# A decoder of two layers on one core: the late stage in groups of four, two and two batches in place of four and four, the second attention's scores in two PSUM banks in place of three

## The reference

```
x = layernorm(x + attn0(x))          # 16 heads of 64, softmax, out projection
x = layernorm(x + xattn0(x, ctx))    # one head of 128, softmax, biases
x = layernorm(x + ffn0(x))           # tokens @ We + be, times the best gate's probability
x = layernorm(x + attn1(x))          # 16 heads of 8, causal softmax, out projection
x = layernorm(x + xattn1(x, ctx))    # rotated q and k, scores * decay mask, no softmax
x = layernorm(x + ffn1(x))           # inner 512, silu(gate) * up, down
```

## Time and profile before

| | |
|---|---|
| median of 3 runs | 333.19 us (332.2 to 333.38) |
| the profiled execution | 330.77 us, its span 329.0 us |
| busy share of the span | TensorE 76%, VectorE 66%, ScalarE 45%, GpSimd 20% |
| mean granted clock of TensorE | 0.902 of full |

### The profile page before, as it was taken

The page is one execution under the profiler, slowest core; times in us unless marked ns, Lnnn a source line. Parts: engine busy times, 40 slices in busy tenths (PEclk is TensorE's granted clock), DMA queues, the critical chain, the costliest instruction groups (busy, mean ns, idle before and its releaser), DMA issues.

```text
span 329.0 us, 6840 instructions
## 1 busy us (share of the span) xinstructions
PE 250.3 (76%) x2655; PEld 190.5 (58%) x2658; DVE 216.4 (66%) x538; ACT 148.2 (45%) x274; POOL 67.0 (20%) x102
## 2 busy tenths in 40 slices
PE   0858688988999989799967899999886667652430
PEld 0836567878787878687845566666564434240110
DVE  3996995679657996865356656567476756354662
ACT  5864662275437736144422354543525552202651
POOL 8900000000011001171114681352020002021002
PEclk9989999999999999999978999999999995655555
DMA  7985541344133502436000620004000000000011
GB/s 235 388 224 165 121 102 66 115 96 114 66 106 88 130 3 85 130 103 100 2 1 0 134 26 2 0 18 90 0 3 2 1 2 0 0 0 1 0 32 32
DMA packets 27679, 22.86 MB, mean 69 GB/s; under 512 B 19136, under 2 KB 24256, under 8 KB 26944
## 3 DMA queue, kind: packets, MB, share of 16 engines
q1 hardware_dynamic: 27648, 22.43, 25.9%
HBM read 12.20 MB, written 6.03 MB: 55 GB/s over the span
## 4 chain that ended last, share of the span: by engine, by line
PE 48%; DVE 28%; ACT 11%; issue 7%; POOL 3%; DMA 1%; ACTq 0%; DVEq 0%; POOLq 0%
DVE arena L1076 7%; PE PS L506 4%; ACT arena L883 3%; PE PS L683 3%; PE PS L579 3%; PE PS L606 3%; ACT xt L906 3%; PE PS L705 2%; DVE rowmax L1081 2%; PE PS L598 2%; PE PS L547 2%; POOL rstd L433 2%; PE PS L689 2%; PE PS L532 2%; PE PS L688 2%
## 5 line engine op out<-in xcount | busy, mean ns | idle before, releaser
L431 POOL TENSOR_SCALAR shift<-mv 128x3 f32<-128x3 f32 (+2 forms) x15 | 3.6, 240 | 243.2 <-DVE mv L1138 243.2
L1076 DVE TENSOR_TENSOR arena<-PS,arena 64x512 f16<-64x512 f32 x64 | 44.1, 690 | 6.7 <-ACT arena L883 5.1
L883 ACT ACTIVATE arena<-PS 64x512 f16<-64x512 f32 x64 | 37.8, 591 | 19.2 <-PE PS L534 18.4
L532 PE MATMUL PS<-xh,w0l 128*128 128x256 f32 x64 | 21.7, 339 | 17.0 <-DVE w0l L1067 9.5
L962 ACT ACTIVATE PT<-PS 128x512 f32<-128x512 f32 x32 | 19.1, 595 | 34.2 <-PE PS L689 34.1
L906 ACT ACTIVATE xt<-res,shift,rstd 128x128 f32<-128x128 f32 x42 | 17.7, 483 | 32.6 <-POOL shift L434 32.5
L1211 DVE TENSOR_REDUCE rowmax<-PS 128x4 f32<-128x512 f32 x32 | 21.9, 688 | 13.5 <-PE PS L691 13.1
L896 ACT ACTIVATE PT<-PS 128x512 f32<-128x512 f32 x32 | 19.1, 597 | 16.0 <-PE PS L563 14.5
L532 PEld LDWEIGHTS PS<-xh,w0l 128*128 128x128 f32 x64 | 13.4, 209 | 19.4 <-DVE arena L1076 9.7
L579 PE MATMUL PS<-V,PT 128*64 128x68 f32 x512 | 22.2, 229 | 1.9 <-DVE On L1105 1.9
L561 PE MATMUL PS<-arena 128*128 128x128 f16 x128 | 23.3, 221 | 0.3 <-DVE MR L1088 0.3
(11 more groups left out here) (206 smaller groups left out, 652.1 us busy)
## 6 DMA issues: line engine op xcount, KB each, us to landing
arena<-arena SPq DMA_DIRECT2D x8, 512.0 KB, 5.1
v_piece<-VN SPq DMA_DIRECT2D x8, 512.0 KB, 2.7
V<-v_piece SPq DMA_DIRECT2D x64, 64.0 KB, 2.5
arena<-k_piece SPq DMA_DIRECT2D x4, 192.0 KB, 4.4
arena<-q_piece SPq DMA_DIRECT2D x4, 192.0 KB, 6.3
q_piece<-VN SPq DMA_DIRECT2D x6, 96.0 KB, 1.7
xT<-x_T SPq DMA_DIRECT2D x1, 512.0 KB, 3.8
w<-wk SPq DMA_DIRECT2D x2, 256.0 KB, 4.6
```

The lines of the kernel that those rows point to most:

```text
L532: mm(dst, w0l[:, w, g], xh[:, x], start=True, stop=False)
L883: m = fn(dst[:, a], src[a * 64:(a + 1) * 64], ACT.Copy)
L1076: m = tt(lower[:, a], src[a * 64:(a + 1) * 64], upper[:, a], ALU.subtract)
```

## The change

Groups 3, 4 and 5 have four, two and two batches. Group 5 (batches 6 and 7) is now the last one, in which half of the batches are normalised by VectorE and the gate uses Silu; group 4 (batches 4 and 5) uses tanh, whose product takes one more VectorE instruction (L1242), and starts when the residuals of its own batches are there, while batches 6 and 7 are in the second attention. Its steps 0 to 11 use one PSUM bank, number 2, in two halves, which is why the scores are left with banks 0 and 1, and why V, which shares its half with K, moves from step 0 to step 2 and waits until VectorE has read K. Its first gate waits for the residual of batch 7. Group 5 uses banks 3 and 4. The buffers of group 4 in SBUF lie in tiles of the first attention and of the weights that are no longer read.

The diff, cut to what it does; each `LBANKS[g][i]` in the late steps becomes `LTILES[g][i]`, each `w % 3` a `w % 2`:

```diff
-N = (3, 3, 2, 4, 4)
-B0 = (0, 3, 6, 0, 4)
+N = (3, 3, 2, 4, 2, 2)
+B0 = (0, 3, 6, 0, 4, 6)
-MIDS, LATES = (0, 1, 2), (3, 4)
+MIDS, LATES = (0, 1, 2), (3, 4, 5)
...
-        LBANKS = {3: (5, 6, 7), 4: (4, 0, 1)}
+        LTILES = {3: (PS[:, 5, :], PS[:, 6, :], PS[:, 7, :]),
+                  4: (PS[:, 2, 0:TP], PS[:, 2, 0:TP], PS[:, 2, TP:2 * TP]),
+                  5: (PS[:, 4, 0:TP], PS[:, 3, 0:TP], PS[:, 3, TP:2 * TP])}
...
         def gate_bank(b):
-            return 6 if b < B0[-1] else 2 * (b % 2)
+            return 0 if b in (4, 6) else 6
...
         def gates_at(g, j):
-            ahead = int(g == LATES[-1])
+            ahead = int(g != LATES[0])
...
-        at = max(at, plan("late", 4, T1 + u1(LAST[4]) + 11, 0, (0, 1), FFN_END[3]))
+        after1 = T1 + u1(NB - 1) + 11, 0
+        at = max(at, plan("late", 4, T1 + u1(LAST[4]) + 13, 0, (0, 1), max(FFN_END[3], after1)))
+        at = max(at, plan("late", 5, *after1, (0, 1), FFN_END[4]))
...
             def scores1(w, b, q, of_keys):
-                if w >= 3:
-                    pe.wait_ge(s1_free[w % 3], w // 3)
+                if w >= 2:
+                    pe.wait_ge(s1_free[w % 2], w // 2)
...
                     else:
-                        pe.wait_ge(s("res1_done"), NB)
+                        pe.wait_ge(s("res1_done"), B0[g] + N[g])
...
-                    tiles(g, part_of(bank(LBANKS[g][0]), g), tokens(cT, g), wx1[:, 4, :], True).then_inc(s("pe_vx1"), 1)
+                if i == (2 if g == LATES[1] else 0):
+                    if g == LATES[1]:
+                        pe.wait_ge(s("k1_mul"), g - 2)
+                    tiles(g, part_of(LTILES[g][0], g), tokens(cT, g), wx1[:, 4, :], True).then_inc(s("pe_vx1"), 1)
...
+                    if g == LATES[1] and j == 0:
+                        pe.wait_ge(s("res1_done"), NB)
...
-                for b in range(B0[g], B0[g] + (2 if g == LATES[-1] else N[g])):
+                for b in range(B0[g], B0[g] + (1 if g == LATES[-1] else N[g])):
...
             def late(g, i):
-                if i == 0:
+                if i == (2 if g == LATES[1] else 0):
                     act.wait_ge(s("pe_vx1"), g - 2)
...
-                    for b in range(B0[g] + 2, B0[g] + 4):
+                    for b in range(B0[g] + 1, B0[g] + N[g]):
```

More of the change, by code:

```diff
@@ L155, in decoder, with three @@
-        hb, th = (ring(two(1536 + i * 1024, 6144, 1024)) for i in range(2))
-        x5q, x5T = (two(7168 + i * 512, 12288, 512, ab) for i in range(2))
-        hi, hT = (ring(two(8192 + i * 1024, 12288, 1024, ab)) for i in range(2))
-        LBANKS = {3: (5, 6, 7), 4: (4, 0, 1)}
+        Onf, OTf = flat(On[:]), OT[:].rearrange("p b g c -> p (b g c)")
+        Onb, wgub = Onf.bitcast(BF16), wgu_s[:].bitcast(BF16)
+        def three(first, offset, n, own, where=af):
+            return {3: where[:, first:first + n], 4: own, 5: where[:, offset + first:offset + first + n]}
@@ new lines, in ring @@
+        def ring(sets):
+            return {g: x.rearrange("p (i c) -> p i c", i=2) for g, x in sets.items()}
+        lA, lC, lD, lE = ({3: x, 4: Onf[:, i * TP:(i + 1) * TP], 5: Vf[:, i * 512:(i + 1) * 512]}
+                          for i, x in enumerate((mA, mC, kx0, vx0)))
+        kx1, vx1, x5r = (three(i * 512, 6144, 512, Onf[:, (4 + i) * TP:(5 + i) * TP]) for i in range(3))
+        hb, th = (ring(three(1536 + i * 1024, 6144, 1024, OTf[:, i * 1024:(i + 1) * 1024])) for i in range(2))
+        x5q, x5T = (three(7168 + i * 512, 12288, 512, Onb[:, 14 * TP + i * TP:14 * TP + (i + 1) * TP], ab)
+                    for i in range(2))
@@ L160, in gate_bank, with late_of @@
+        hi, hT = (ring(three(8192 + i * 1024, 12288, 1024, wgub[:, i * 1024:(i + 1) * 1024], ab))
+                  for i in range(2))
+        LTILES = {3: (PS[:, 5, :], PS[:, 6, :], PS[:, 7, :]),
+                  4: (PS[:, 2, 0:TP], PS[:, 2, 0:TP], PS[:, 2, TP:2 * TP]),
+                  5: (PS[:, 4, 0:TP], PS[:, 3, 0:TP], PS[:, 3, TP:2 * TP])}
+        def late_of(b):
+            return LATES[(b >= B0[4]) + (b >= B0[5])]
         def gate_bank(b):
-            return 6 if b < B0[-1] else 2 * (b % 2)
+            return 0 if b in (4, 6) else 6
@@ L198, in decoder @@
         pj_free = [sem("pj_free0"), sem("pj_free1")]
-        s1_free = [sem(f"s1_free{i}") for i in range(3)]
+        s1_free = [sem(f"s1_free{i}") for i in range(2)]
         block = ctx.enter_context(nc.Block())
@@ L632, in mid @@
                     pe.wait_ge(s("kx0"), g + 1)
-                    turn_x(g, 0, 6)
+                    turn_x(g, 0, bank(6))
                 if i == 4:
@@ L649, in mid @@
                 if i == 12:
-                    turn_x(g, 1, 7)
+                    turn_x(g, 1, bank(7))
                 if i == 13:
@@ L659, in mid @@
                 if i == 18:
-                    turn_x(g, 2, 6)
+                    turn_x(g, 2, bank(6))
                 if i == 19:
@@ L921, in mid @@
                 if i == 3:
-                    copy_x(g, 0, 6)
+                    copy_x(g, 0, bank(6))
                 if i == 4:
@@ L934, in mid @@
                 if i == 12:
-                    copy_x(g, 1, 7)
+                    copy_x(g, 1, bank(7))
                 if i == 14:
@@ L941, in mid @@
                 if i == 18:
-                    copy_x(g, 2, 6)
+                    copy_x(g, 2, bank(6))
                 if i == 19:
```

88 lines of the change are left out of this document (41 added, 47 removed).

## The result

The kernel with the change takes **338.14 us**, the median of 4 runs (337.2 to 338.34); the kernel before took 332.69 on the same occasion (4 runs, 332.2 to 333.38). The ratio is **1.0177, with a 95% interval from 1.0133 to 1.0221**: the change makes the kernel 1.8% slower. The profiled execution of the new kernel took 338.12 us, its span is 336.3 us.

A forecast was written before the change was run, and what follows sets the result against it. After about 271 us no engine is full; short instructions wait in turn across engines. Terms 0.8 + 11.8 - 8.3 = +4.3 us took the profiled execution from 330.77 to 335.1; with 2.4 for the median, 337.5, range 331.0 to 342.5.

The forecast's parts named there:

- the likeliest case: Whole kernel: slower, 337.5 us, own range 334.5 to 341; chance 0.58.
- Part 1: Second attention: two score banks for three make scores wait for late maxima and exponentials; +0.8 us, from 0 to about 3.
- The late maximum of tick 20: Second attention: row maximum ends at 215.75, queries' scores had started at 215.44; few late maxima cost about 0.4 us.
- the fast ticks: Second attention: exponential ends 0.10 us before the next scores of keys start, about seven times; about 0.4 us.
- Part 2: Ticks 35 to 40: group 4's steps delay batch 7's residual by 11.8 us; bounds 1.3 and 15.
- its upper bound: Ticks 35 to 40: 15 us if TensorE falls to half clock in idle stretches 274.5 to 276.6 and 278.7 to 281.6.
- Part 3: Tail after batch 7's residual, last group with two batches: -8.3 us, bounds -12 and -5.
- The bound from above: Tail: saves only 5 us if group 5's steps wait out one more product, 2.6, and its residual and hand-offs.
- the sum of +4.3: Whole kernel: 0.8 + 11.8 - 8.3 on the profiled span of 329.0 us.
- Faster: Ticks 35 to 40: group 4 fits into the waits, front costs 4.7, change -2.8, so 330.4 us; chance 0.15.
- The clock: Tail: two interleaved groups keep TensorE at full clock after 283, giving back 3.4, so 334.1 us; chance 0.14.
- Much slower: Front at half clock and bank waits at their upper bound: 15 + 3 - 8.3 = +9.7, so 343 us; chance 0.13.

The follow-up runs named there:

- group 4 behind the attention: The changed kernel, but group 4's steps start in tick 41 and behind, together with group 5's, instead of ticks 35 to 40: 332.05 us, ratio 0.9992.
- the same work in another order: The changed kernel with V made in step 0 and group 4's steps 2 to 11 queued behind group 3's: 332.72 us, ratio 0.9999.
- V free: The changed kernel with group 4's V made in step 0 with K, in its own bank 5: 338.40 us, ratio 1.0186.

## Why the prediction was right, step by step

- **The forecast.** 337.5 against 338.14, inside the range, slower as the likeliest case said. The mechanism is the one predicted, and the experiments bear it out: the early placement alone makes the loss (group 4 behind the attention), and what makes it is that group 4's steps stand ahead of the others in the queues (the same work in another order). That the two times are 0.6 apart is in part luck, see the base below.
- **Part 1.** +0.8 is close to the 0.6 that the traces show, but it is made up of other waits. The late maximum of tick 20 came, 0.36, and was taken up by the next waits; the fast ticks cost nothing. What stayed is the wait of the first scores of keys in tick 5, 0.4 to 0.5, which the prediction doesn't name, and 0.17 in tick 31. The time can't tell 0.6 from nothing (ratio 1.000).
- **Part 2.** All three steps came in the predicted places: the rounding of batch 0 behind a normalisation, +4.34 beside the residual of batch 5 (predicted 4.3); the gate of batch 2 behind the second normalisation, +11.4 (9.8); batch 7's outputs directly behind the quantisation, +13.3 (11.8). The term was sized too small by 1.9, and it was priced at full clock. The clock was named in its upper bound, but put in idle stretches after 274; it fell earlier as well, at about 264.7. The kernel with added matmuls shows about 2 us less up to batch 6. That the whole 1.9 is the clock is argued, not shown: that kernel lost it again before batch 7.
- **One reason inside it was incomplete.** The prediction blamed V's shared half for the first 4.3 together with the normalisation. With V free the loss stays the same to 0.01; the root's wait is enough for all of it.
- **Part 3.** -8.3 against -8.96, and its terms -0.75, -6.4, -1.15 against -1.02, -6.45, -1.24. (The parts that it gives for the last of these, 0.8, 1.7 and 0.5, add up to the 3.0 measured, not to its 3.1.) The start came 0.37 later than assumed and the stores 0.62 sooner. Group 4's products stood where it had put them, batch 4's ahead of group 5's decay (302.18, decay at 304.65) and batch 5's ahead of the quantisation (310.52, 313.27). The bound from above, that group 5 waits out another product, didn't happen.
- **The base.** The prediction set the sum of +4.3 against the median, by taking 2.4 for the distance of the profiled execution before. The terms measured against it give 13.72 - 8.96 = 4.8, and the medians 5.45. The rest is within the scatter of single executions (329.45 to 334.14 in 22 of 23 runs of the kernel before). The change was forecast about 1.1 too small. The forecast time is nearer than that because its base, 333.19 from three runs, stood 0.5 above the 332.69 of the comparison; the medians of 23 and 17 runs are lower still, 332.24 and 332.07.
- **Its signs.** The residual of batch 7 was to come near 284 and came at 287.73: 1.9 of that is the front, the rest the later start. The ticks up to 33 were to be under 2 us late and were 2.4 to 2.5 late from tick 6 on (2.7 in tick 20), mostly from ahead of tick 5, which no term of the sum covers. From the last turned input to the last residual it was 12.65, within the 12 to 13 given.
- **The rivals.** *Faster* needed a front under 5.8; it was 13.7. Its argument from group 3 leaves out that there no feed-forward stood behind the waits, as the prediction itself objected; no run tries this by itself. The same work behind the others' steps instead of ahead of them took 5.7 back, and still was not faster than before. *The clock* in the tail: 0.50 in 290 to 300, 0.67, 0.50, 0.50 in the next three stretches of ten; the denser tail didn't hold it. *Much slower*: its half clock in the front did come, for some 2 us of the 3.2 it priced; of its 3 us of bank waits 0.6 came.

## What to carry to other kernels

Before moving a group of work into "idle" time, go through each engine's queue and write down what stands behind each of its waits. A step that waits for another engine's answer holds everything behind it; here the same steps, placed behind the others, cost 5.7 us less. When a wait is named by the trace, look for a second one right behind it before removing the first. And look for a seam where the halves of a split group meet: joined into one row, with group 3's last normalisation moved ahead, the split took 1.7% off the kernel before, where as two rows it took nothing.

## What the runs showed of the hardware

- The granted clock fell to half in the middle of the attention, at about 264.7, behind 3.30 us in which TensorE waited, though the matmuls of V began again at 263.42 and those of the scores at 264.42. In the kernel before it was 1.00 from 255 to 271, and with 14 added matmuls in that wait it stayed at 1.00. The wait was thus paid twice here: the four turnings that took 0.66 in the kernel before (at 258.35) took 1.12 here (at 266.79), and a pair of gate matmuls 0.85 in place of 0.59.
- The added matmuls were no free remedy: 12 of 512 columns took 4.82, mostly at half clock, and held real work for 2.3.
- A third score bank was worth about 0.6 us in the traces, at two places of the second attention, and nothing that the times can show (ratio 1.000, 0.9973 to 1.0026).
- A table load on ScalarE took 1.28. It started 0.05 behind the last normalisation (313.07 + 1.64, then 314.76), and the first Silu 0.02 behind it (316.06). Taking it off the path gave 1.28 in the profile. The Trainium skill (ScalarE: Activation LUTs, section "What ACT_TABLE_LOAD costs") gives 2.66 for a switch, a drain of 1.38 with it. No such drain shows in these rows, and the measurement decides: 1.3 is what a switch cost here.
